# Cross-attention on one core: the value products of three items issued together in the third item's step

## The reference, cut to what matters

```python
q = x @ Wq.T                                   # 32 heads of 16, RMS-normed
k_raw, v_raw = context @ Wk.T, context @ Wv.T  # 375 rows; k RMS-normed
scores = jnp.einsum('bhnd,bhmd->bhnm', q, k) * scale
attn = jax.nn.softmax(scores, axis=-1)
out = jnp.einsum('bhnm,bhmd->bhnd', attn, v)
```

## Time and profile before

| what | us |
|---|---|
| median of three runs | 900.78 (900.61 to 901.1) |
| the profiled execution, its own time | 900.3 |
| its span, first to last instruction | 898.5 |
| TensorE busy | 885.5 (99%) |
| VectorE busy | 596.1 (66%) |
| ScalarE busy | 464.4 (52%) |
| GpSimd busy | 204.8 (23%) |

### The profile page before, as it was taken

The page is one execution under the profiler, slowest core; times in us unless marked ns, Lnnn a source line. Parts: engine busy times, 40 slices in busy tenths (PEclk is TensorE's granted clock), DMA queues, the critical chain, the costliest instruction groups (busy, mean ns, idle before and its releaser), DMA issues.

```text
span 898.5 us, 17919 instructions
## 1 busy us (share of the span) xinstructions
PE 885.5 (99%) x7088; PEld 778.1 (87%) x7088; DVE 596.1 (66%) x1304; ACT 464.4 (52%) x1119; POOL 204.8 (23%) x147
## 2 busy tenths in 40 slices
PE   8999999999999999999999999999999999999995
PEld 8998989898989899877788888888877898999994
DVE  7886566666666635675665656646557878888883
ACT  5543333333333344547766666666675336656551
POOL 0143232323232215301101111011000621132233
PEclk9999999999999999999999999999999999999998
DMA  6221242424212115040200001000043688989973
GB/s 225 66 94 42 78 141 80 138 84 135 85 64 90 47 47 181 28 137 1 84 24 25 13 24 37 13 24 14 1 167 123 243 303 302 358 283 305 297 206 47
DMA packets 42195, 104.56 MB, mean 116 GB/s; under 512 B 8208, under 2 KB 18560, under 8 KB 40192
## 3 DMA queue, kind: packets, MB, share of 16 engines
q1 hardware_dynamic: 37808, 94.23, 30.7%
q0 software_dynamic: 4304, 9.19, 5.0%
HBM read 75.57 MB, written 18.65 MB: 105 GB/s over the span
## 4 chain that ended last, share of the span: by engine, by line
PE 96%; DVE 2%; ACT 0%; issue 0%; DMA 0%; POOL 0%; DVEq 0%
PE bank L595 25%; PE bank L596 24%; PE bank L597 24%; PE bank L852 5%; PE bank L869 5%; PE bank L695 3%; PE bank L671 3%; PE bank L683 1%; PE bank L711 1%; PE bank L812 1%; PE bank L981 1%; PE bank L879 1%; PE bank L989 1%; DVE pp L1745 0%; PE bank L819 0%
## 5 line engine op out<-in xcount | busy, mean ns | idle before, releaser
L1380 ACT ACTIVATE ee<-bank 125x448 f32<-125x448 f32 x192 | 90.8, 546 | 13.6 <-PE bank L852 13.6
L1628 DVE TENSOR_TENSOR E_lo<-F,E_hi 128x940 fp32r<-128x940 f32 (+3 forms) x62 | 80.8, 1320 | 2.2 <-ACT E_hi L1147 2.1
L595 PE MATMUL bank<-wkv_hi,ctx_hi 128*125 128x512 f32 x192 | 79.9, 416 | 0.0
L2330 POOL TENSOR_TENSOR ctx_lo<-ctx_f,ctx_hi 128x500 fp32r<-128x500 f32 x24 | 30.6, 1276 | 204.2 <-ACT ctx_hi L1147 204.2
L596 PE MATMUL bank<-wkv_hi,ctx_lo 128*125 128x512 f32 x192 | 76.2, 397 | 0.0
L597 PE MATMUL bank<-wkv_lo,ctx_hi 128*125 128x512 f32 x192 | 75.8, 395 | 0.0
L1147 ACT ACTIVATE E_hi<-F 128x940 fp32r<-128x940 f32 (+3 forms) x62 | 67.9, 1140 | 7.9 <-PE bank L597 3.6
L2330 POOL TENSOR_TENSOR wqk_lo<-wqk_f,wqk_hi 128x1024 fp32r<-128x1024 f32 x14 | 35.1, 2507 | 155.5 <-ACT wqk_hi L1147 155.5
L2440 POOL DMA_INDIRECT out<-yg,meta x21 | 39.5, 1880 | 126.1 <-DMA out<-yg,meta 72.1
L595 PE MATMUL bank<-wv_hi,xT_hi 128*128 128x256 f32 x224 | 63.5, 283 | 0.1
L597 PE MATMUL bank<-wv_lo,xT_hi 128*128 128x256 f32 x224 | 62.6, 279 | 0.0
(11 more groups left out here) (411 smaller groups left out, 2571.3 us busy)
## 6 DMA issues: line engine op xcount, KB each, us to landing
F<-wexp SPq DMA_DIRECT2D x14, 1408.0 KB, 7.7
F<-wexp SPq DMA_DIRECT2D x14, 768.0 KB, 6.9
wqk_f<-wqk SPq DMA_DIRECT2D x16, 512.0 KB, 4.3
ctx_f<-ctx SPq DMA_DIRECT2D x24, 250.0 KB, 2.8
slots<-zt SPq DMA_DIRECT2D x3, 1799.0 KB, 8.1
xg<-slots SPq DMA_DIRECT2D x21, 256.0 KB, 7.4
wv_f<-wv SPq DMA_DIRECT2D x8, 512.0 KB, 5.5
wo_f<-wo SPq DMA_DIRECT2D x8, 512.0 KB, 3.5
```

The lines of the kernel that those rows point to most:

```text
L595: e.matmul(out, a[0], b[0], start=first, stop=False)
L1380: e.activation(ee[(4 * n + r) % 8][:, :], SX[r][0:MS, 0:4 * T], ACT.Exp, scale=0.25).then_inc(*x_exped.did((n, r)))
L1628: return e.tensor_tensor(out, src, high.bitcast(F32), ALU.subtract)
L2330: return e.tensor_tensor(out, src, high.bitcast(F32), ALU.subtract)
```

## The change

In the third step the value products of all three items of the unit are issued together; the first step has none. For this the exponentials have 12 tiles (`NEE`) and the values 7 (`NVB`); the added tiles lie in the room "z", which the last self-attention projection reads until just before. GpSimd sets the ones and zeros of the seventh value tile in step 0, ahead of the small split of the gate weights. ACT's waits are moved by one item: exponentials of item `n` wait for the products of `n - 3`, not `n - 2`, and value rows of item `k` for those of `k - 7`, not `k - 6`.

```diff
+NEE, NVB = 4 * MC, 7
...
-        ee = [sbl(f"ee{i}", [MS, 4 * T], F32, "mid" if i < 6 else "z") for i in range(8)]
+        ee = [sbl(f"ee{i}", [MS, 4 * T], F32, "mid" if i < 6 else "z") for i in range(NEE)]
+        vb.append(sbl("vb6", [MS, XH, VW], F32, "z"))
...
             def value_pe(n):
...
-                w.wait_ge(*consts_set["one", 11])
+                w.wait_ge(*consts_set["one", 11 if n < NVB - 1 else 2 * NVB - 1])
...
-                        i = e.matmul(AB[32 * c:32 * c + VW, r * T:(r + 1) * T], vb[n % 6][:, 8 * (c // 2) + 2 * r + c % 2, :],
-                                     ee[(4 * n + r) % 8][:, c * T:(c + 1) * T], start=m == 0 and r == 0,
+                        i = e.matmul(AB[32 * c:32 * c + VW, r * T:(r + 1) * T], vb[n % NVB][:, 8 * (c // 2) + 2 * r + c % 2, :],
+                                     ee[(4 * n + r) % NEE][:, c * T:(c + 1) * T], start=m == 0 and r == 0,
...
                 if m == MC - 1:
-                    value_pe(n - 1)
-                if m != 1:
-                    value_pe(n)
+                    for k in range(n - 2, n + 1):
+                        value_pe(k)
...
-                    if k > 5:
-                        w.wait_ge(*valued[k - 6, 3])
+                    if k >= NVB:
+                        w.wait_ge(*valued[k - NVB, 3])
...
             def score_exp(n, r):
                 w.wait_ge(*scored_x[n, r])
-                if n > 1:
-                    w.wait_ge(*valued[n - 2, r])
+                if n >= MC:
+                    w.wait_ge(*valued[n - MC, r])
...
                 if n == 0:
+                    w.wait_ge(*pj_full["o", NH // 2 - 1, NA - 1])
+                    ones(NVB - 1)
                     w.wait_ge(*gw_hi[0])
```

More of the change, by code:

```diff
@@ L479, in decoder_layer @@
         padded = lane("pad", [0])
-        consts_set = sig("consts_set", ["eps1", "zt", "zn", "eps"] + [("one", i) for i in range(12)] + [("route", i) for i in range(NE + NRB + 2)])
+        consts_set = sig("consts_set", ["eps1", "zt", "zn", "eps"] + [("one", i) for i in range(2 * NVB)] + [("route", i) for i in range(NE + NRB + 2)])
         mv_done = {n: sig(f"mv{n}", range(k)) for n, k in ((1, NA), (2, NB), (3, NB))}
@@ L1362, in rows_square @@
                     k = keys.index((u, m))
-                    if k > 5:
-                        w.wait_ge(*valued[k - 6, 3])
-                    w.wait_ge(*consts_set["one", 3 if k < 2 else 11])
-                    e.activation(vb[k % 6][:, :, 0:16], KB[n % 2][0:MS, 256:512].rearrange("p (h d) -> p h d", d=16),
+                    if k >= NVB:
+                        w.wait_ge(*valued[k - NVB, 3])
+                    w.wait_ge(*consts_set["one", 3 if k < 2 else 11 if k < NVB - 1 else 2 * NVB - 1])
+                    e.activation(vb[k % NVB][:, :, 0:16], KB[n % 2][0:MS, 256:512].rearrange("p (h d) -> p h d", d=16),
                                  ACT.Copy).then_inc(*squared.did(((u, m), "v")))
@@ L1377, in score_exp @@
                 w.wait_ge(*scored_x[n, r])
-                if n > 1:
-                    w.wait_ge(*valued[n - 2, r])
-                e.activation(ee[(4 * n + r) % 8][:, :], SX[r][0:MS, 0:4 * T], ACT.Exp, scale=0.25).then_inc(*x_exped.did((n, r)))
+                if n >= MC:
+                    w.wait_ge(*valued[n - MC, r])
+                e.activation(ee[(4 * n + r) % NEE][:, :], SX[r][0:MS, 0:4 * T], ACT.Exp, scale=0.25).then_inc(*x_exped.did((n, r)))
             def value_copy(u):
```

## The result

| | us |
|---|---|
| before, median of six runs | 900.84 |
| changed, median of six runs | 907.79 (907.41 to 908.74) |
| ratio | 1.0079, 95% interval 1.0066 to 1.0092 |
| span of the profiled execution | 906.9 (before 898.5) |

The change makes the kernel 7 us slower. The page of the changed kernel: busy times, and the chain by engine (compare).

A forecast was written before the change was run, and what follows sets the result against it. TensorE, busy 99% of the span, was taken as the bound. Third steps' 12.3 us less 5.3 us gained gave +7.0: execution 900.3 to 907.3, median 0.5 above, 907.8; range 904.5 to 910.8.

The forecast's parts named there:

- First step: Each unit's first step loses its 32 value instructions, so TensorE's work there gets 0.92 us shorter.
- Third step: Each unit's third step takes 32 more value instructions: 0.77 us a unit, 12.3 us in 16 units.
- `kn` does not move: Normed key rows come no sooner, so second steps' row products wait; the first step's gain shrinks to 5.3 us.
- about 0.85: New TensorE wait predicted in an even unit's second step, in us; about 0.28 in an odd one.
- 14 second steps: The number of second steps in which the prediction said TensorE now waits.
- Signal time: From DVE's signal to TensorE's start: 0.06 us taken; 0.10 instead would cost +0.5 us.
- Restart: Unhidden weight load behind a wait: taken as nothing, at most 0.18 us in 14 units, up to +2.5 us.
- The sum: Third steps' 12.3 us less the 5.3 us gained makes +7.0 us; median 907.8.
- rival 3: Waits in 14 second steps put TensorE's clock to its lower level: 48 us lost, 955; chance 0.02.
- rival 2: Chain to `kn` 0.4 to 0.5 us shorter in 14 units, needing the root before the queries' square: 901.5; chance 0.06.
- the estimate of +5.2: Sum in us, instead of +7.0, if GpSimd's split moved away from DVE's instruction in five even units.

The follow-up runs named there:

- Experiment 11: Changed kernel with `kn` made earlier by reordered ACT and DVE, context splits a step ahead except tile 6's: 900.44 us, ratio 0.9996.
- experiment 9: Changed kernel with `kn` made earlier by reordered ACT and DVE, context splits of even units a step before their first: 906.75 us, ratio 1.0066.
- Experiments 4 to 10: Seven runs reordering ACT and DVE or moving the context split, on the changed kernel or the kernel before: 906.55 to 912.60 us.
- experiment 5: Changed kernel with one context tile's split moved from even units' first step to their second: 909.37 us.
- experiment 7: Changed kernel with `kn` made earlier by reordered ACT and DVE, context split in the second step: 906.55 us, ratio 1.0071.
- experiments 2 and 3: Changed kernel with item 0's products in the second step, 902.79 us; and with each item's products in its own step, 904.96 us.
- experiment 10: Kernel before, products in old places, with `kn` made earlier by reordered ACT and DVE, context splits a step ahead: 908.41 us, ratio 1.0089.
- experiments 4 and 6: Changed kernel with `kn` made earlier on ACT and DVE, 912.60 us; and with only DVE's sum before the norm, 908.23 us.

## Why the prediction was right, by its steps

- **First step.** Forecast 0.92 less; measured 0.89 to 0.92, in unit 6 0.91 (6.88 to 5.97). From turn to scores it is 507.04 - 506.73 = 0.31, not 0.29.
- **Third step.** Forecast +0.77; measured 2.44 - 1.67 = 0.77; 12.2 us in 16 units, forecast 12.3.
- **`kn` does not move.** It ends 8.16 us after the first step's scores in unit 6, 8.15 before; 7.8 in the odd units as before. The row products are 0.26 to 0.28 us late in units 3 to 13 odd, forecast 0.28, and 0.89 to 0.91 in the even units 4 to 14. For those the prediction's "about 0.85" is the 0.92 less the whole slack; its own sum, which leaves 0.06 for the signal, comes to about 0.9. Experiment 11 shows the other side: move it, and the loss is gone.
- **How many waits.** The prediction speaks of 14 second steps. Its own list has 15 (units 0 to 14), and 15 wait. The sum goes by the list and is not touched.
- **Signal time.** Forecast 0.06 with 0.10 as the other end; measured 0.05 to 0.06 in 15 waits. So the 0.06 us that units 1, 8 and 14 had before was no slack.
- **Restart.** Forecast nothing, at most 0.18 a wait; the second matmul of L597 starts 0.80 us behind the first with the wait (509.29, 510.09) and without (506.41, 507.21).
- **The sum.** Stage: forecast 12.3 - 5.3 = +7.0, measured 12.15 - 4.94 = +7.2; first and second steps together gained a little less than forecast. Two units take 537.52 - 501.07 = 36.45 us, forecast 36.4. Median: forecast 907.8, measured 907.79. That the second is so near is partly luck: the profiled execution is the slowest of the six and 8.4 longer in span; 7.2 are in this stage, and 1.0 lies between TensorE's last matmul (starts at 888.59 before, 896.00 after) and the end of the last stores.
- **Clock.** Granted 1.00 in the stage as before, with TensorE waiting in each second step but the last; rival 3 has nothing for it here. By "A second HAM failure mode: psum-queue depth-cycling" of the Trainium skill's page TensorE: Matmul & The Clock Gate it might have switched; this case's trace does not agree for waits of this length. It was no empty rival, though: in the 5.08 us of TensorE's idle time in experiment 9 the clock fell to its lower level.

```profile
501.07:537.70 36.63, 35.84 (x437) 28.97 (x437) 21.25 (x69) 23.47 (x67) 3.79 (x3) 1.00 0.09 23
```

Busy times of one batch (compare; the stretch is 0.18 us longer than the two units): 35.84 of 36.63 us are busy, at a clock of 1.00.

What was not right, beside the forecast, is rival 2's remark on what a shorter chain needs. It named the root before the queries' square alone. Experiments 4 to 10 show that it also takes DVE's copy of the turned keys, the norm, GpSimd's split and a load in their right places. And the estimate of +5.2 if the split moved away did not come true in experiment 5: the split held up another instruction.

## What to carry to other kernels

Work on the bound engine that stands between a producer's input and its consumer is cover, even if it has nothing to do with them: before moving it, read the distance from the last signal to the instruction behind it, for each kind of step, and count the move's gain only up to that slack. Putting the same work back into another step costs nearly its full length (0.77 of 0.91 us here), so a saving of 0.14 us on paper can turn into a loss of 0.45 a unit. And an engine with a written-out order passes a delay on, even one that is only 66% busy like DVE here: after each edit look for the next instruction that was just in time. Where a long wait appears, read the granted clock behind it before the whole loss is put down to the wait.

## What the runs showed of the hardware

- A group of small value products costs 0.13 to 0.30 us beside its own work (0.77 us for 32), by its neighbours: 0.13 to 0.14 right in front of the scores (0.90 - 0.77 before the change; joining saves 0.11 to 0.15 in experiment 7's odd units), about 0.30 between a turn and full-size matmuls or another turn (1.07 and 1.06 - 0.77, experiments 2 and 3).
- TensorE's waits of up to 0.91 us, one in about 18 us, left the granted clock at 1.00 (the changed kernel, 15 times). In an idle time of 5.08 us (experiment 9) and one of 5.17 us (experiment 10) the granted clock fell to 0.50, and it stayed there for some 5 and 3.5 us more in which TensorE was busy throughout.
- A GpSimd tensor operation of 1.25 or 1.26 us held up different DVE instructions: one on 112 x 1 took 1.03 us instead of 0.12, one on 112 x 512 took 1.44 instead of 0.55. The first ended within 0.02 us of GpSimd's, the second 0.28 after it. A sum over 125 x 256 that ran beside such a split kept its 0.42 us (experiments 4 and 6).
